# A state-space layer in the middle of a two-layer kernel: the transfers of its head, the staging, one gated output and three orders of work are rearranged

## The reference, cut to what matters

```python
proj = hidden_states @ in_proj_w.T                 # 512 -> 8192 gate, 10240 xBC, 128 dt
gate, xBC, dt = jnp.split(proj, [INTER, INTER + CONV_DIM], axis=-1)
xBC = silu(causal_conv4(xBC, conv_w) + conv_b)     # then x [128 heads x 64], B, C [8 groups x 128]
dt = clip(softplus(dt + dt_bias), 0.001, 100)
cs = cumsum(dt * A)                                # in chunks of 128 tokens
Lmat = where(tri, exp(cs_l - cs_s), 0)
y = (C B^T * Lmat) @ (x * dt) + state passed between chunks + x * D
yg = y * silu(gate)
out = (yg * rsqrt(mean(yg**2 over the 1024 channels of a group) + eps)) * norm_w
return out @ out_proj_w.T
```

## Time and profile before

| | us |
|---|---|
| median of 3 runs (lowest, highest) | 2398.34 (2393.13, 2399.88) |
| the profiled execution | 2399.32 |
| its span in the profile | 2397.5 |
| mean granted clock of TensorE | 0.951 |
| busy: PE, DVE, ACT, POOL | 2188.8, 1550.0, 1192.4, 811.7 |

### The profile page before, as it was taken

One profiled execution on the slowest core, in us unless ns is written; L12 is line 12 of the kernel. 1 busy time (PEld: TensorE's weight loads), 2 busy tenths in 40 slices (PEclk: granted clock), 3 DMA queues, 4 the chain that ended last, 5 costly groups with the idle time before them and its releaser, 6 DMA issues. The chain is left out here.

```text
span 2397.5 us, 38308 instructions
## 1 busy us (share of the span) xinstructions
PE 2188.8 (91%) x11176; PEld 1606.8 (67%) x11176; DVE 1550.0 (65%) x3186; ACT 1192.4 (50%) x2846; POOL 811.7 (34%) x680
## 2 busy tenths in 40 slices
PE   6798888898599999999999999999999999987998
PEld 4554544444477777777777687777777777766876
DVE  3555655653478578768758858857857876855345
ACT  3453444411367457556646736636745754653230
POOL 4342432311034324424414524433432542431220
PEclk8698998898799999999999999999999999988999
DMA  5000000001699469549729839937937954812100
GB/s 234 10 1 1 10 1 1 1 1 59 119 252 235 85 168 233 137 128 228 181 86 223 195 87 216 226 79 181 237 84 170 234 134 126 200 40 88 52 10 36
DMA packets 242900, 286.96 MB, mean 120 GB/s; under 512 B 9344, under 2 KB 211328, under 8 KB 242048
## 3 DMA queue, kind: packets, MB, share of 16 engines
q1 hardware_dynamic: 242688, 284.43, 49.2%
HBM read 281.78 MB, written 104.60 MB: 161 GB/s over the span
## 5 line engine op out<-in xcount | busy, mean ns | idle before, releaser
L1670 PE MATMUL b_ps<-xh_keep,wh 128*128 128x512 f32 x1152 | 475.0, 412 | 14.1 <-DVE xdt L1477 13.3
L1671 PE MATMUL b_ps<-xl_keep,wh 128*128 128x512 f32 x1152 | 457.1, 397 | 0.0
L1672 PE MATMUL b_ps<-xh_keep,wl 128*128 128x512 f32 x1152 | 456.7, 396 | 0.0
L1468 DVE TENSOR_TENSOR decayed<-b_ps,b_scores 128x384 f32<-128x384 f32 x512 | 282.1, 551 | 149.6 <-ACT b_ps L1193 148.4
L1442 DVE SCALAR_TENSOR_TENSOR xs<-b_ps,par,xs 128x510 f32<-128x510 f32 (+2 forms) x384 | 284.8, 742 | 58.7 <-ACT xs L1164 44.2
L1353 POOL TENSOR_TENSOR wl<-wraw,wh 128x512 fp32r<-128x512 f32 x144 | 186.7, 1297 | 338.9 <-ACT wh L1143 338.9
L1670 PEld LDWEIGHTS b_ps<-xh_keep,wh 128*128 128x128 f32 x1152 | 217.3, 189 | 93.9 <-issue 45.5
L1672 PEld LDWEIGHTS b_ps<-xh_keep,wl 128*128 128x128 f32 x1152 | 217.5, 189 | 52.3
L1671 PEld LDWEIGHTS b_ps<-xl_keep,wh 128*128 128x128 f32 x1152 | 217.7, 189 | 44.0
L1192 ACT ACTIVATE b_ps<-rows,ncs 128x256 f32<-128x256 f32 x512 | 237.1, 463 | 17.4 <-DMA rows<-skewed_rows 8.6
L1753 PE MATMUL b_ps<-oh,yh 128*128 128x512 f32 x512 | 207.6, 405 | 25.1 <-DVE yl L1560 25.1
(11 more groups left out here) (222 smaller groups left out, 3989.0 us busy)
## 6 DMA issues: line engine op xcount, KB each, us to landing
rows<-skewed_rows SPq DMA_DIRECT2D x256, 384.0 KB, 4.8
skewed_rows<-sum_rows SPq DMA_DIRECT2D x64, 1024.0 KB, 11.0
wraw<-win_dram SPq DMA_DIRECT2D x144, 256.0 KB, 5.2
skewed_rows<-sum_rows SPq DMA_DIRECT2D x64, 512.0 KB, 12.9
oraw<-wout_dram SPq DMA_DIRECT2D x8, 2048.0 KB, 9.2
w<-w_dram SPq DMA_DIRECT2D x2, 3584.0 KB, 23.1
fraw<-wgu_dram SPq DMA_DIRECT2D x11, 512.0 KB, 3.4
draw<-wd_dram SPq DMA_DIRECT2D x1, 2816.0 KB, 11.5
```

Of the source, the lines that this page charges most:

```text
L1468: nc.vector.tensor_tensor(sd[:, b, h, :], ps[bk.bank(ph, name)][:, 0:ROW], sm[:, b, :], ALU.mult)\
L1670: nc.tensor.matmul(out, w_h, x_h, start=(k == 0), stop=False)
L1671: nc.tensor.matmul(out, w_h, x_l, start=False, stop=False)
L1672: last = nc.tensor.matmul(out, w_l, x_h, start=False, stop=(k == KT - 1))
```

## The change

Six things are moved; the arithmetic is the same.

- Staging 0 is issued per sequence: `stage_first(b)` for b = 3, 0, 1, 2, two DMAs each, with semaphores of their own. `load_rows(0, b)` waits for those of b and of b − 1.
- SP's head: slices 6 and 7 come right behind `stage_first`, then all four rows of unit 0, then `stage(1)` to `stage(4)`. In the loop stagings 5 to 8 of a group are issued at j = 0, 2, 4, 6, and the next group's 1 to 4 at its end. `load_out` moves from j = 0 to j = 1. The semaphores of staging go from 4 to 8.
- Output 0 of a group is cut into its parts in the units instead of the crossing: weights and half 1 at the end of unit 5, half 0 at the end of unit 6 (ACT, DVE), the weights' lo part in unit 6 (POOL).
- The order in `steps`: on ACT the tanh of G{j}_1 comes before both exponentials of sequence 3, in unit 0 the first exponential comes before the tap; on DVE the silu of that gate half comes before the decay and `skip(j-1, 0)`, in unit 0 the first decay comes before the taps and scores 2 and 3.
- `times_dt(j, 1)` comes right behind `times_dt(j, 0)`.
- PE's head: C1 and X0_0 are made before the cumulated sums, X0_1 before they are turned.

```diff
@@ -1036,7 +1036,8 @@
         dt_loaded, par_loaded, padded, kept = (sem(f"d_{n}") for n in ("loaded", "par", "padded", "kept"))
-        staged = [sem(f"staged{k}") for k in range(4)]
+        staged = [sem(f"staged{k}") for k in range(8)]
+        first_staged = [sem(f"first_staged{b}") for b in range(BATCH)]
         dt_split, sums_ready = sem("d_split"), sem("d_sums")
@@ -1058,6 +1059,14 @@
                     .then_inc(o_loaded.sem, 16)
+
+            def stage_first(b):
+
+                src, dst = ssm["rows"].tensor, ssm["skewed"].tensor
+                for at, shift, cols in ((0, 0, SEQ), (SEQ, P, P)):
+                    sp.dma_start(bass.AP(tensor=dst, offset=b * ROW + at, ap=[[WIDE + 1, P], [BATCH * ROW, 2], [1, cols]]),
+                                 bass.AP(tensor=src, offset=b * ROW + shift, ap=[[1, P], [BATCH * ROW, 2], [1, cols]]))\
+                        .then_inc(first_staged[b], 16)
@@ -1071,7 +1080,7 @@
                                  bass.AP(tensor=src, offset=s0 + shift, ap=[[1, P], [ROW, 2 * BATCH], [1, cols]]))\
-                        .then_inc(staged[n % 4], 16)
+                        .then_inc(staged[n % 8], 16)
@@ -1081,7 +1090,10 @@
                     sp.wait_ge(*bk.filled(ph, f"E{j}_{b}_1"))
-                sp.wait_ge(staged[n % 4], 32 * (n // 4 + 1))
+                    sp.wait_ge(staged[n % 8], 32 * ((n - 1) // 8 + 1))
+                else:
+                    for k in (b - 1, b):
+                        sp.wait_ge(first_staged[k % BATCH], 32)
                 sp.dma_start(rows[:, b], bass.AP(tensor=ssm["skewed"].tensor, offset=n % STAGED * P * WIDE + b * ROW,
@@ -1100,22 +1112,25 @@
             sp.wait_ge(kept, 16)
-            stage(0)
-            for b in range(BATCH - 1):
-                load_rows(0, b)
-            stage(1)
-            stage(2)
+            for b in (BATCH - 1, *range(BATCH - 1)):
+                stage_first(b)
             load_in(0, 6)
             load_in(0, 7)
+            for b in range(BATCH):
+                load_rows(0, b)
+            for n in range(1, 5):
+                stage(n)
             for g in range(NG):
...
                         load_in(g, 8 + 2 * j)
-                    load_rows(n, BATCH - 1)
-                    stage(n + 3)
-                    if not j:
+                    if n:
+                        load_rows(n, BATCH - 1)
+                    if j % 2 == 0:
+                        stage(g * UNITS + 5 + j // 2)
+                    if j == 1:
                         load_out(g)
@@ -1125,6 +1140,8 @@
                     load_in(g, SUBS + 7)
+                    for k in range(1, 5):
+                        stage((g + 1) * UNITS + k)
@@ -1230,12 +1247,15 @@
                     if j:
-                        next(before)
                         tanh(ph, conv_halves(j)[3])
                         next(before)
+                        next(before)
+                    else:
+                        next(now[0])
                     if h:
                         tap(ph, gn, h[0], f"Y{j - 1}_0" if j and not final else None)
-                    next(now[0])
+                    if j:
+                        next(now[0])
                     if more:
@@ -1259,6 +1279,11 @@
                         square(ph, j - 1, 1)
+                    if j == LAST - 2:
+                        out_weights_hi(ph, g, 0)
+                        out_hi(ph, g, 0, 1)
+                    if j == LAST - 1:
+                        out_hi(ph, g, 0, 0)
@@ -1272,12 +1297,9 @@
                 square(ph, LAST, 0)
-                out_weights_hi(ph, g, 0)
                 tap(ph, g + 1, h[1], f"Y{LAST - 1}_1")
                 weights_hi(g, SUBS + 5)
-                out_hi(ph, g, 0, 1)
                 tanh(ph, h[0])
-                out_hi(ph, g, 0, 0)
                 square(ph, LAST, 1)
@@ -1332,11 +1354,8 @@
             steps(ph, LOOPS, True)
-            out_weights_hi(ph, LOOPS, 0)
-            out_hi(ph, LOOPS, 0, 1)
             for _ in exps(ph, LOOPS, LAST, 3):
                 pass
-            out_hi(ph, LOOPS, 0, 0)
             square(ph, LAST, 0)
@@ -1387,6 +1406,8 @@
                         add_square(ph, j - 1, 1)
+                    if j == LAST - 1:
+                        out_weights_lo(g, 0)
@@ -1396,7 +1417,6 @@
                 add_square(ph, LAST, 0)
-                out_weights_lo(i, 0)
                 gate(ph, LAST, 1)
@@ -1404,7 +1424,6 @@
             steps(ph, LOOPS, True)
-            out_weights_lo(LOOPS, 0)
             gate(ph, LAST, 0)
@@ -1464,6 +1483,8 @@
                         dve.wait_ge(*(bk.filled(ph, f"Y{j - 1}_{b // 2}") if b % 2 else scanned.made(ph, (j - 1, b))))
+                    if not j and not h:
+                        dve.wait_ge(*(bk.freed if b < 2 else bk.drained)(ph, f"CB{2 + b % 2}"))
                     dve.wait_ge(*bk.filled(ph, name))
@@ -1501,24 +1522,27 @@
                     if j:
+                        silu(ph, conv_halves(j)[3])
                         next(before)
                         skip(ph, g, j - 1, 0)
-                        silu(ph, conv_halves(j)[3])
                         next(before)
+                    else:
+                        next(now[0])
                     if h:
                         taps(ph, gn, h[0], (1, 2))
-                    next(now[0])
+                    if j:
+                        next(now[0])
+                    else:
+                        scores(ph, 2)
+                        scores(ph, 3)
                     if h:
...
                     next(now[0])
-                    if not j:
-                        scores(ph, 2)
-                        scores(ph, 3)
                     times_dt(ph, g, j, 0)
+                    times_dt(ph, g, j, 1)
                     if h:
...
                     next(now[1])
-                    times_dt(ph, g, j, 1)
                     if j:
@@ -1534,6 +1558,8 @@
                         taps(ph, gn, h[2])
+                    if LAST - 2 <= j < LAST:
+                        out_lo(ph, g, 0, LAST - 1 - j)
@@ -1548,10 +1574,8 @@
                 taps(ph, g + 1, h[1])
-                out_lo(ph, g, 0, 1)
                 silu(ph, h[0])
                 silu(ph, h[2])
-                out_lo(ph, g, 0, 0)
                 silu(ph, h[1])
@@ -1647,12 +1671,10 @@
             steps(ph, LOOPS, True)
-            out_lo(ph, LOOPS, 0, 1)
             for _ in decays(ph, LAST, 3):
...
             skip(ph, LOOPS, LAST, 1)
-            out_lo(ph, LOOPS, 0, 0)
             project(ph, LOOPS)
@@ -1782,6 +1804,8 @@
             in_half(ph, 0, 1, bc_[2])
+            in_half(ph, 0, 1, bc_[3])
+            in_half(ph, 0, 2, h[0])
             pe.wait_ge(dA_done, 1)
@@ -1794,7 +1818,7 @@
                     last.then_inc(*bk.full(ph, name))
-            in_half(ph, 0, 1, bc_[3])
+            in_half(ph, 0, 2, h[1])
             for t in range(NT):
@@ -1803,8 +1827,8 @@
                     last.then_inc(*bk.full(ph, name))
-            for q, name in enumerate(h):
-                in_half(ph, 0, 2 + q // 2, name)
+            for name in h[2:4]:
+                in_half(ph, 0, 3, name)
             first_scores(ph)
```

## The result

The changed kernel takes 2417.72 us in the median of 6 runs, the kernel before 2399.11 in the 6 runs beside it. The ratio is 1.0094, with a 95% interval of 1.0074 to 1.0113: slower by 22 us, or by 18 to 27; the two medians lie 19 us apart. The forecast was 2404, range 2379 to 2417. The median is 14 us above the one and 0.7 above the other, on the side of rivals 3 and 4.

The account below looks back on a forecast made before the run. PE, busy 91%, was taken as the bound, with a transfer-bound stretch in the head. Head +6.6, group 0 +0.3, groups 1 to 6 −3.6, last group +2.2 made +5.5 on 2399.32; median forecast 2404, range 2379 to 2417.

Parts of the forecast that it names:

- rival 3: Units and crossing: half clock already sets in behind PE waits above about 1 us, +12 to 14 us, 2417; chance 0.18.
- rival 4: Head: each of staging 0's eight DMAs pays a fixed part, 8.5 us later, 2412; chance 0.08.
- (i): Crossing: PE's wait and half clock at output 0 go, a new 0.9 us wait at ms is safe; −4.0 us.
- (d): Units: ACT's tanh ahead of the exponential lengthens the ACT-DVE loop from 15.99 to 16.46 us, six units a group, +2.9.
- (f): Units 5 and 6: output 0's copies moved in from the crossing delay ACT, +1.27 and then +0.15 us.
- (e): Units: moving times_dt(j,1) up gains nothing, since its scan's input comes no sooner.
- (g): Units: staging spread over j = 0, 2, 4, 6 and the group's end costs nothing, as rows are staged five ahead.
- (h): Unit 0: scores 2 and 3 behind the first decay remove PE's 0.92 us wait, −0.9 in every group but the first.
- rivals 1 and 2: Units: order swap costs nothing, 2381, chance 0.19. Head: rows(1,0) isn't held up, 2377, chance 0.10.

Follow-up runs that it names:

- e1: Changed kernel with the ms matmuls at the crossing moved behind two more output tiles; 2404.69 us, ratio 1.0014 to the kernel before.
- e4: Changed kernel with output 0 cut into its parts in the crossing again, as before; 2427.38 us, ratio 1.0096 to the kernel before.
- e8: Kernel before with only the two orders of steps (ACT's tanh, DVE's silu) changed; 2418.47 us, ratio 1.0075 to the kernel before.
- e9: Kernel before with only the cut of output 0 moved into units 5 and 6; 2397.97 us, ratio 1.0006 to the kernel before.
- e3: Changed kernel with SP's program as before, PE's new head kept; 2404.97 us, ratio 1.0007 to the kernel before.
- e2: Changed kernel with the two orders of steps put back for units 1 to 7; 2403.64 us, ratio 1.0012 to the kernel before.
- e12: Changed kernel with the ms matmuls moved behind one more output tile; 2413.37 us, ratio 1.0065 to the kernel before.
- e5: Changed kernel with the mends of e1, e2 and e3 together; 2370.44 us, ratio 0.9863 to the kernel before.
- e6: e5 with output 0's copies and lo part moved into ACT's and DVE's waits inside units 5 and 6; 2347.23 us, ratio 0.9780 to the kernel before.
- e7: e6 with SP's queue in group 0 reordered, fewer stagings ahead of rows(1,0), six output weights loaded early; 2332.61 us, ratio 0.9716 to the kernel before.
- e10: e7 with C1 and X0_0 put back behind the cumulated sums on PE; 2334.00 us, ratio 0.9725 to the kernel before.
- e11: e7 with unit 0's order and times_dt(j,1) as in the kernel before; 2339.63 us, ratio 0.9757 to the kernel before.

## Why the prediction failed, point by point

**The clock at the crossing (7.8 us of the miss).** Step (i) said that a new wait of 0.9 is safe, because the clock was 1.00 behind the 0.92 in the earlier trace rows, and took all seven half-clock stretches away. The wait came as forecast (1.09), and half clock followed in 4 of 7 groups, five stretches of 3.4 us. That was rival 3, put at 0.18 and at the right place. Its 2417 is the measured time only by luck: of the 12 us or more that it put on the clock some 8 came, none of them in the units, and the head made up most of the rest. Shown: e1 takes the wait away and all stretches go. The error was to carry one row, at another place, over to this one. (By the prediction's own numbers the wait was 993.0 − 992.2 = 0.8, not 0.9.) The count over the kernels here, of output projections with half clock, by the wait ahead of it:

| kernel | wait at the crossing, us | half clock |
|---|---|---|
| before, e4, e8 | 3.2 to 3.4 | 7 of 7 |
| e9 | 0.93 | 6 of 7 |
| e3 | 1.1 | 6 of 7 |
| after, e2 | 1.1 | 4 of 7 |
| e12 | 0.44 | 2 of 7 |
| e1, e5, e6, e7, e10, e11 | none at `ms` | 0 of 7 |

In e8 five of the seven stretches begin only behind the second wait, of some 0.55 at `ms`. What tells the groups of one kernel apart is not settled; their waits are equal to 0.03 us. Nor is it shown why the wait at `ms` does it and the one at the turning of X doesn't: behind the first stand the `ms` matmuls of 128x1, for 1.9 us, behind the second 128x128 ones, and no run parts the wait from what follows it. The Trainium skill ("TensorE: Matmul & The Clock Gate", section "Why this matters for your kernels") asks for gaps under about 3 us; here the clock fell behind waits of 0.44 to 1.1, so the trace is stricter.

**The head (4.2 us).** The queue was priced rightly and started wrongly. From rows(0,0) to rows(1,0) the sum had 51.1 us; the five profiles with this head (the changed kernel, e1, e2, e4, e12) show 51.2 to 54.4. But the start, 632.45 for the end of staging 0, was SP's next issue in the earlier trace rows; the rows it issued reached ACT 3.8 us later, and I charged them 1.3. That term was 2.5 us short. Of rival 4, eight DMAs for two, 1.4 us are left: from the first staging's issue to rows(0,0) at ACT pass 18.76 us (637.30 − 618.54), before 15.67 (638.27 − 622.60); of the 3.1 more the two slices ahead are 1.7. What is left is far under the 12 us that the prediction worked out from the Trainium skill ("DMA: Bandwidth & Descriptors", section "Anatomy of one DMA — SWDGE (gpsimd) path"). The Trainium skill gives 2 us there for one DMA, fitted on those that GpSimd issues, while SP issues these; that each further DMA in a row pays it again in full was the prediction's step. Over the five profiles the head is 111.6 us on the mean, against 99.1 in the three with the head of before (the kernel before, e8, e9): 12.5, twice the forecast 6.6. With 9.6 for the rest, which is from one profile each, this makes 22, as the ratio has it, where this one profile showed 18; both lie within the ratio's interval.

**The units (1.4 us) and the last group (1.5).** The period of (d) was exact, 16.46, and e2 and e8 show it from both sides; but five periods of a group turn in that loop (e8), where six were counted. (f) was right for unit 5 (1.37 over the new unit, 1.27 forecast) and mis-sized for the one behind: 16.91 instead of 15.70, +1.21 where 0.48 + 0.15 were put down, partly given back at the crossing. Alone, in e9, the copies cost 1.24 and 1.21, together 2.45 a group, where (f) had 1.42: the one sum's excess hid most of the other's lack. e6 shows that the copies' cost was a matter of place. The last group's 1.5 us have no experiment of their own.

**Right:** the wait at the first product gone; the `ms` wait in its place; PE's long wait moved from the turning of X to unit 1 (9.4 us of it are left there, not 2: counted from the layer's first matmul, PE is out of work 3.7 us sooner, and the turning starts 3.4 later than worked out, since rows(0,0) came late as above); (e), (g) and (h) (e11: 7.2 us for unit 0's order, 6.3 forecast); that rivals 1 and 2 would not come.

Put together, and read from the profiles, the change holds two parts that help (output 0, 7.5 us beside the other parts, nothing alone; unit 0's order, 7, taken out of e7_drain), two that cost 20 and 12 (the two orders of steps; SP's head, which costs 14 between the means of the profiles that have PE's new head, 97.7 in e3, e5 and e6 and 111.6 in the five), and PE's head, worth 2 at most.

## What to carry to other kernels

Find the loop that sets the period and ask of each moved instruction whether it stands on that loop or in a wait of its engine: the same copies of output 0 cost 2.4 us a group at one place and nothing 9 us earlier. In a queue that drains in order, count the bytes ahead of the transfer that the next step needs; prefetching further ahead is a cost there. A new small wait on PE is not priced by its length alone: put a few matmuls of other work in front of a late input where that is possible.

## What the runs showed of the hardware

Half clock behind a wait of 0.44 us, in 2 groups of 7 with equal waits, and none behind two waits of 1.00 and 0.96 us 17 us apart (e5): a single wait's length is no sure guide in either direction. The untouched first layer differs by 9.5 us between profiles of kernels whose code for it is the same (578.4 to 587.9), which is more than the 0.3% that a median resolves; a change of this size has to be read from a mark inside the profile. The clock goes with that difference. Here is layer 0 in e7_drain and in e2_order:

```profile
0.00:578.40 578.40, 482.08 (x2480) 276.51 (x2480) 308.66 (x1074) 234.76 (x818) 184.72 (x213) 0.90 0.08 28
0.00:587.90 587.90, 491.19 (x2481) 283.20 (x2481) 308.92 (x1075) 235.19 (x818) 185.13 (x213) 0.88 0.07 28
```

Added up over the trace's records of the clock, the first is at half clock for 112 us, the second for 136, and the kernel before, at 586.3, for 133. Half of the 24 us between the first two is 12, enough for the 9.5. Why the clock falls more often in one execution is open. The drain of DRAM-to-DRAM stagings at full engines repeated within 6% (51.2 to 54.4 us for five and their rows), well enough to order a queue by arithmetic.
